# Conv attention: the first head's conv taps made on VectorE instead of ScalarE and GpSimd

## The reference

```python
Q = (query @ Wq.T + bq).reshape(b, s, h, dh).transpose(0, 2, 1, 3)
K = (query @ Wk.T + bk).reshape(b, s, h, dh).transpose(0, 2, 1, 3)
V = (query @ Wv.T + bv).reshape(b, s, h, dh).transpose(0, 2, 1, 3)
scores = jnp.einsum('bhqd,bhkd->bhqk', Q, K) / np.sqrt(dh).astype(np.float32)
x = scores.transpose(0, 2, 1, 3).reshape(b * s, h, s)
x = lax.conv_general_dilated(x, conv_w, window_strides=(1,), padding=[(KS // 2, KS // 2)], dimension_numbers=('NCW', 'OIW', 'NCW'))
x = x + conv_b[None, :, None]
scores = x.reshape(b, s, h, s).transpose(0, 2, 1, 3)
weights = jax.nn.softmax(scores, axis=-1)
out = jnp.einsum('bhqk,bhkd->bqhd', weights, V).reshape(b, s, e)
return out @ Wo.T + bo
```

## Time and profile before

| | us |
|---|---|
| median of three runs | 4256.34 |
| lowest and highest of them | 4252.75, 4263.25 |
| the profiled execution, its own time | 4279.9 |
| its span, first to last instruction | 4278.1 |

### The profile page before, as it was taken

How to read it: one execution, slowest core, us unless ns; L and a number is a source line. 1 busy time by engine, 2 the same in 40 slices (tenths; PEclk the granted TensorE clock), 3 DMA queues, 4 the chain that set the end, 5 groups by cost and what they waited for, 6 DMA issues and landing times. The chain is left out here.

```text
span 4278.1 us, 65347 instructions
## 1 busy us (share of the span) xinstructions
PE 3577.1 (84%) x22240; PEld 2809.3 (66%) x22240; DVE 2966.4 (69%) x6077; ACT 2680.0 (63%) x3510; POOL 2104.9 (49%) x1157
## 2 busy tenths in 40 slices
PE   6877524156999999999999999996788888679999
PEld 4545311134777777777777777774567666679999
DVE  4567777875877887778877878885666666544347
ACT  3344446765877878778777878883667566333443
POOL 0044310005766667667676767770666666371004
PEclk9989756578999999999999999997899999789999
DMA  1057500005877878778877878884367477633224
GB/s 46 0 111 131 109 1 0 0 1 141 151 138 134 148 134 144 137 140 142 141 138 135 148 134 153 150 152 86 70 109 142 84 131 122 190 114 97 75 78 140
DMA packets 1571358, 470.18 MB, mean 110 GB/s; under 512 B 1507174, under 2 KB 1565159, under 8 KB 1569767
## 3 DMA queue, kind: packets, MB, share of 16 engines
q1 hardware_dynamic: 1564903, 449.40, 55.3%
q0 software_dynamic: 6144, 16.79, 1.2%
HBM read 49.00 MB, written 39.58 MB: 21 GB/s over the span
## 5 line engine op out<-in xcount | busy, mean ns | idle before, releaser
L2116 DVE TENSOR_REDUCE d_neg_max<-psum 128x1 f32<-128x1024 f32 x512 | 625.3, 1221 | 337.0 <-PE psum L1857 334.2
L2003 ACT ACTIVATE psum<-psum,d_bias 128x1024 f32<-128x1024 f32 x512 | 558.2, 1090 | 384.3 <-DVE d_bias L2120 383.5
L1857 PE MATMUL psum<-d_KH,d_QH 128*128 128x512 f32 x2048 | 682.7, 415 | 13.5 <-POOL d_KL L1824 7.8
L1857 PE MATMUL psum<-d_KL,d_QH 128*128 128x512 f32 x2048 | 638.1, 393 | 0.0
L1857 PE MATMUL psum<-d_KH,d_QL 128*128 128x512 f32 x2048 | 636.8, 392 | 0.0
L2125 DVE SCALAR_TENSOR_TENSOR d_halves<-psum,d_halves 128x1024 f16<-128x1024 f32 x512 | 622.6, 1216 | 14.8 <-ACT d_halves L2010 13.9
L2010 ACT ACTIVATE d_halves<-psum 128x1024 f16<-128x1024 f32 x512 | 520.6, 1017 | 3.2
L1824 POOL TENSOR_TENSOR d_KL<-d_KC,d_KH 128x1024 fp32r<-128x1024 f32 x128 | 307.3, 2401 | 338.7 <-ACT d_KH L1999 338.7
L1857 PEld LDWEIGHTS psum<-d_KH,d_QH 128*128 128x128 f32 x2048 | 362.6, 188 | 141.3 <-issue 73.3
L1857 PEld LDWEIGHTS psum<-d_KL,d_QH 128*128 128x128 f32 x2048 | 385.2, 188 | 86.9
L1857 PEld LDWEIGHTS psum<-d_KH,d_QL 128*128 128x128 f32 x2048 | 385.2, 188 | 86.7
(11 more groups left out here) (474 smaller groups left out, 7742.6 us busy)
## 6 DMA issues: line engine op xcount, KB each, us to landing
f_weights_raw<-in_L_ffn_packed_dram SPq DMA_DIRECT2D x10, 1088.0 KB, 15.7
f_tile<-expert_rows SPq DMA_DIRECT2D x71, 128.0 KB, 2.1
f_expert_out<-f_tile SPq DMA_DIRECT2D x71, 128.0 KB, 1.7
d_probsT<-d_halves SPq DMA_TRANSPOSE x512, 4.3
f_tile<-f_kept_rows SPq DMA_DIRECT2D x64, 128.0 KB
expert_rows<-d_group_mixT SPq DMA_DIRECT2D x7, 1024.0 KB, 11.4
residual_stream<-in_x_dram SPq DMA_DIRECT2D x4, 1024.0 KB, 9.5
f_kept_rows<-residual_stream SPq DMA_DIRECT2D x4, 1024.0 KB, 8.1
```

The source lines that it names most:

```text
L1857: last = t.matmul(scores_at(u)[:, cols], q_part[:, ch, j * P:(j + 1) * P], k_part[hh % 2][:, ch, cols], start=k == 0, stop=k == 5)
L2003: a.activation(scores_at(u), scores_at(u), ACT.Exp, bias=bias[u % 2][:, 0:1])\
L2116: v.tensor_reduce(neg_max[u % 2][:], scores_at(u), AXIS.X, ALU.max, negate=True)\
```

## The change

The first head's taps (head 0 of sequence 0, both chunks) are made by DVE alone. It waits for the keys, then issues two TENSOR_SCALAR for the middle tap and four SCALAR_TENSOR_TENSOR (keys times factor plus what stands in `KC`) for the outer ones, ahead of the query moves. The last two count up `tap_three`, so that ACT's `high` and POOL's `low` follow as before. POOL skips `add_taps(0)` and begins with `low(0)`. ACT drops its four taps of head 0 and has `high(0, 0)` and `high(0, 1)` ahead of all eight `queries`, where they stood between and behind them. The counters `tapped`, `tap_one` and `tap_two` begin with head 1, so their numbers are shifted; from head 1 on every engine's list is the one of before. PE's and SP's lists are unchanged.

```diff
                 def add_taps(hh):
                     b, h = hh // H, hh % H
                     for ch in range(DC):
-                        at = DC * hh + ch + 1
+                        at, seen = DC * hh + ch + 1, DC * (hh - 1) + ch + 1
...
-                        g.wait_ge(tap_one.sem, tap_one.at(at))
-                        g.wait_ge(tapped.sem, tapped.at(2 * at - 1))
+                        g.wait_ge(tap_one.sem, tap_one.at(seen))
+                        g.wait_ge(tapped.sem, tapped.at(2 * seen - 1))
...
                 for hh in range(H * B):
                     b, h = hh // H, hh % H
-                    add_taps(hh)
+                    if hh:
+                        add_taps(hh)
                     low(hh)
...
                     if h == 0:
                         a.wait_ge(k_ready.sem, k_ready.at(4 * b + 4))
-                    if hh:
-                        a.wait_ge(tap_three.sem, tap_three.at(DC * (hh - 1) + ch + 1))
+                    a.wait_ge(tap_three.sem, tap_three.at(DC * (hh - 1) + ch + 1))
...
-                for ch in range(DC):
-                    for k in (0, 2):
-                        tap(0, ch, k)
+                high(0, 0)
+                high(0, 1)
                 for j in range(TB):
                     queries(0, j)
-                    if j == 3:
-                        high(0, 0)
-                high(0, 1)
                 tap(1, 0, 0)
                 tap(1, 0, 2)
                 values(0, 0, 0)
...
+                v.wait_ge(k_ready.sem, k_ready.at(4))
+                v.wait_ge(cleared.sem, cleared.at(5))
+                for ch in range(DC):
+                    v.tensor_scalar(KC[:, ch, :], K[0][:, ch, 1:S + 1], taps[:, ch, 1:2], None, ALU.mult)\
+                        .then_inc(first_taps.sem, 1)
+                for ch in range(DC):
+                    v.wait_ge(first_taps.sem, first_taps.at(ch + 1))
+                    v.scalar_tensor_tensor(KC[:, ch, :], K[0][:, ch, 0:S], taps[:, ch, 0:1], KC[:, ch, :], ALU.mult,
+                                           ALU.add).then_inc(first_taps.sem, 1)
+                for ch in range(DC):
+                    v.wait_ge(first_taps.sem, first_taps.at(DC + ch + 1))
+                    v.scalar_tensor_tensor(KC[:, ch, :], K[0][:, ch, 2:S + 2], taps[:, ch, 2:3], KC[:, ch, :], ALU.mult,
+                                           ALU.add).then_inc(tap_three.sem, 1)
                 for k in range(4):
                     move_queries(0, k, PS[:, (4 + k) * BANK:(5 + k) * BANK])
```

More of the change, by code:

```diff
@@ L1686, in stage_conv_attention @@
     tap_three = c("tap_three")
+    first_taps = c("first_taps")
     key_high = c("key_high")
@@ L1810, in add_taps @@
                                         ALU.mult).then_inc(tap_one.sem, 1)
-                        g.wait_ge(tap_one.sem, tap_one.at(at))
-                        g.wait_ge(tapped.sem, tapped.at(2 * at - 1))
+                        g.wait_ge(tap_one.sem, tap_one.at(seen))
+                        g.wait_ge(tapped.sem, tapped.at(2 * seen - 1))
                         g.tensor_tensor(KC[:, ch, :], KC[:, ch, :], tap_of[0][:, ch, :], ALU.add)\
                             .then_inc(tap_two.sem, 1)
-                        g.wait_ge(tap_two.sem, tap_two.at(at))
-                        g.wait_ge(tapped.sem, tapped.at(2 * at))
+                        g.wait_ge(tap_two.sem, tap_two.at(seen))
+                        g.wait_ge(tapped.sem, tapped.at(2 * seen))
                         g.tensor_tensor(KC[:, ch, :], KC[:, ch, :], tap_of[1][:, ch, :], ALU.add)\
@@ L2251, in stage_conv_attention @@
         k.passed(TB * B)
-    tapped.passed(2 * DC * H * B)
-    for k in (tap_one, tap_two, tap_three, key_high, key_low):
+    first_taps.passed(2 * DC)
+    tapped.passed(2 * DC * (H * B - 1))
+    for k in (tap_one, tap_two):
+        k.passed(DC * (H * B - 1))
+    for k in (tap_three, key_high, key_low):
         k.passed(DC * H * B)
```

## The result

| | kernel before | changed kernel |
|---|---|---|
| median of 22 runs each, us | 4254.57 | 4261.96 |
| lowest and highest | 4249.5, 4263.25 | 4252.24, 4267.59 |
| ratio to before, 95% interval | | 1.0014 (1.0008 to 1.0021) |

The forecast was 4251.7, a gain of 4.65 us. The change costs 0.14% instead: too little to matter, but with the wrong sign, and the interval leaves out 1.

What follows compares the result with a forecast made beforehand. PE is 99% busy behind the first score, so only its wait in the opening could shrink. Earlier start 3.65, clock 0.5 and L2171 0.5 sum to 4.65 us off 4256.34: 4251.7 us, range 4245 to 4259.

Steps and rivals of the forecast that it cites:

- The step that failed: From 1027.45 to 2925, where PE is 99% busy, the stretch keeps its length; only the first score comes earlier.
- one of the signs that I had named for being wrong: The stretch behind the first score changes its length by more than 2 us.
- something else moves: Rival: later waits and clock changes fall differently when the stage is shifted, by several us either way; 8%.
- 3.65 forecast: In the opening, PE starts the scores at 1023.8 instead of 1027.45, 3.65 us earlier.
- The taps: DVE's six new opening instructions: middle 0.65, outer 1.20 to the next start; chunk 0 done at 1011.6, chunk 1 at 1012.8.
- `KL`: POOL's subtraction of both chunks in the opening, 4.65 us, ends at 1017.4 instead of 1027.2.
- the held query rests: In the opening, `QL` issues on DVE at 1016.0 and is held by POOL's second `KL` until 1017.4.
- the 6.13 us behind them: From the end of the holding POOL instruction to the end of DVE's last value move: 6.13 us, so `v_ready` at 1023.55.
- the 0.26 that it needed behind POOL: PE's time from release to its first score in the opening, 0.26 us after POOL's second `KL` ended.
- The clock's 0.5: With a shorter wait before the first scores, PE's clock may stay up or return sooner: 0.5 us gained.
- L2171's 0.5: The first value rest on DVE, no longer held by POOL's L1817, takes 1.22 instead of 1.90: 0.5 us gained.
- The lock: A two-input DVE instruction does not run beside a two-input POOL one: `QL` at 1503.38 takes 1.51 instead of 0.42.

Runs made afterwards that it cites:

- The version with a wait of 0.85 us instead of 4.23: Changed kernel with merged memsets (DVE's list at the old positions) and, in the opening, value moves ahead of most query rests, against the kernel before: ratio 0.9999.

## Why the prediction was wrong, point by point

- **The step that failed:** "The change touches nothing in the long stretch, so all that it can bring is an earlier first score: the stretch keeps its length and moves as a whole." It grew by 2.8 us (1897.6 to 1900.4), which was one of the signs that I had named for being wrong. The orders were the same from head 1 on; the positions in DVE's list were not, and seven entries were enough to put the 0.35 us stall on one of three multiplications with 0.20 us to spare. That alone takes back 3.6 us, all that the opening won. I had a case for "something else moves", at 8%, without a mechanism.
- The opening: 3.65 forecast, 3.59 measured in the first pair of profiles, 3.5 to 3.6 in the repeats. The taps, `KL`, the held query rests and the 6.13 us behind them all came out. That it fits to 0.06 is partly luck: `KL` came 0.29 later than forecast (1022.46, where 1017.4 + 4.77 is 1022.17), because POOL began at 1017.77 and not at 1017.47; and PE started 0.05 behind the last value move, where I had put the 0.26 that it needed behind POOL.
- The clock's 0.5 was not there: from the first score to the first maximum it took 5.27, where it had taken 5.22, at a granted clock of 0.55 both times. The version with a wait of 0.85 us instead of 4.23 did keep the high clock (its first matmul pair took 0.73, and 1.22 in the changed kernel).
- L2171's 0.5 came: 1.22 for 1.90, and the first 32 maxima took 111.8 instead of 112.3.
- The lock held as the rows had shown: a two-input POOL add holds a two-input DVE instruction. I used it for the opening and did not look for it in the 128 mix multiplications. One reading of it was off without changing the sum: in the trace of before the 0.84 us that L1809 holds the query rests falls on the third rest (issued at 1015.02, 1.25 long instead of 0.41), and not on the first two.

The sum of the parts to the last maximum is -3.6 - 0.5 + 3.6 - 0.3 for small ones: 1944.7 against 1945.5 in the first pair, 0.8 less than before. To the stage's end the three profiles of each average 1980.6 against 1979.5, 1.1 more, because the tail behind the last maximum is longer: 36.1, 36.1 and 35.3 against 33.6, 35.2 and 33.6. There the clock differs, before:

```profile
2925.06:2932.00 6.94, 2.65 (x24) 1.68 (x20) 4.79 (x9) 2.77 (x4) 0.00 (x0) 0.85 0.89 167
...
2952.00:2958.61 6.61, 4.72 (x20) 3.24 (x18) 1.38 (x2) 0.00 (x0) 0.00 (x0) 1.00 0.00 0
```

and after:

```profile
2928.99:2936.00 7.01, 2.85 (x24) 1.97 (x20) 4.79 (x9) 2.78 (x4) 0.00 (x0) 0.66 0.89 167
...
2956.00:2965.11 9.11, 7.22 (x20) 4.68 (x19) 1.38 (x2) 0.00 (x0) 0.00 (x0) 0.67 0.01 2
```

The clock fell 4.9 to 5.2 us behind the start of the last maximum in the three profiles of the kernel before and 2.1 to 2.3 in those of the changed one. Counted from the first score the fall came at the same place, 1902.5 to 1902.6, in all six: the stretch had grown and the fall had not moved with it. What ties it there no run tested. Nor does the moment of the fall fix the tail's length, since one and the same program, the changed kernel with DVE's list at the old positions, had a tail of 32.3 once and 36.2 once. That leaves 1.1 us seen within the stage, of the 7.4 us between the first medians, and of ratios that mean 6, 1 and 4 us. So the failed step accounts for the gain that did not come; that the changed kernel is slower at all is not explained. The rest stays open: the other stages' lengths vary by more from one execution to the next (the first by 9 us, the last by 29), and the kernel before differed from itself by 0.0009.

## What to carry to other kernels

Before counting a moved or added instruction at its own price, look for the tightest races behind it: pairs on DVE and POOL that read two tensors from SBUF and miss each other by a few tenths of a microsecond. Adding entries to an engine's list shifts where its small stalls fall in everything unrolled behind it; when a stage that wasn't touched changes its length, compare the start of each instruction in both traces, and test with entries that do nothing. An effect of 0.1% is judged by distances in the trace, with the unchanged kernel run against itself for scale.

## What the runs showed of the hardware

- DVE starts some instructions late at fixed entries of its list: mix multiplications by 0.35 us at 3869 and 4509 in the three programs with that length (five profiles), and at 4637 and 5277 in the one five entries shorter; maxima by 0.25 us at 4765 and 5917 in the kernel before. All six entries differ by multiples of 128, and the same instructions are on time when the list ahead is longer or shorter. The other entries of that series show no delay.
- A DVE multiplication of 64 columns took 2.27 instead of 0.23 us when POOL's two-input add had begun 0.15 us ahead of it, and 0.22 when that add came later.
- In the wait of 2.5 us PE's clock fell in the changed kernel's trace at 1518 (0.83 over 1515 to 1525), and the 32 units took 3.6 us more; in the kernel before with seven entries more the same wait passed at 1.00 and cost 2.4.
- The two TENSOR_SCALAR, whose source starts at the second column of the keys, took 0.75 us each, as L1623 does in the earlier trace rows; the four SCALAR_TENSOR_TENSOR of 1024 columns took 1.28, with 1.20 from one start to the next.
